# Where a two-layer kernel issues its small transfers: head loads in parts, divisions a step earlier, residual traffic on GpSimd's queue

## The reference

```
xn = layernorm(x)
s  = attention(xn)            # 32 heads of 16, 8 key/value heads (4 query heads share one), full softmax over 512 keys, then Wo
g  = silu(W_down(fwht(silu(W_gate(f)) * W_up(f) )))    # f = fwht(xn * signs); hidden size 2048
x  = x + s * g
```

## Time and profile before

| | |
|---|---|
| median of 3 runs | 1369.06 us (1363.61 to 1372.95) |
| profiled execution: time, span | 1365.89 us, 1364.1 us |
| mean granted PE clock | 0.986 |
| PE busy | 1249.3 us (92%) |
| DVE busy | 1046.7 us (77%) |
| ACT busy | 785.3 us (58%) |
| POOL busy | 524.1 us (38%) |
| issues from SP in layer 0 | 128 transposes, 128 + 128 head loads, 16 `xres` loads, 16 `x1` stores |

### The profile page before, as it was taken

One profiled execution on the slowest core, in us unless ns is written; L12 is line 12 of the kernel. 1 busy time (PEld: TensorE's weight loads), 2 busy tenths in 40 slices (PEclk: granted clock), 3 DMA queues, 4 the chain that ended last, 5 costly groups with the idle time before them and its releaser, 6 DMA issues. The chain is left out here.

```text
span 1364.1 us, 23475 instructions
## 1 busy us (share of the span) xinstructions
PE 1249.3 (92%) x8738; PEld 642.2 (47%) x8738; DVE 1046.7 (77%) x1823; ACT 785.3 (58%) x1306; POOL 524.1 (38%) x434
## 2 busy tenths in 40 slices
PE   4877898989998998899869999999999999999998
PEld 2332333334333433333324546855486555855475
DVE  6778876878876887789864985878776976868846
ACT  4776776668865887578546552365334652355431
POOL 3699951113201221123112762237331772228431
PEclk9989999999999999999989999999999999999999
DMA  6765554676677766777973024002311024001121
GB/s 235 225 144 98 100 98 82 132 154 129 125 128 159 136 118 131 154 141 131 219 216 139 13 59 82 25 24 60 49 46 40 9 71 83 18 31 48 36 41 47
DMA packets 346561, 135.59 MB, mean 99 GB/s; under 512 B 312176, under 2 KB 333392, under 8 KB 343888
## 3 DMA queue, kind: packets, MB, share of 16 engines
q1 hardware_dynamic: 334032, 132.52, 43.5%
q10 hardware_dynamic: 12416, 1.57, 1.1%
HBM read 44.87 MB, written 17.87 MB: 46 GB/s over the span
## 5 line engine op out<-in xcount | busy, mean ns | idle before, releaser
L1178 PE MATMUL bank<-rows,both 128*128 128x512 f16 x1024 | 241.6, 381 | 18.5 <-DVE th L665 9.8
L954 ACT ACTIVATE probs<-vpair,top_n 128x512 f16<-128x512 f32 x256 | 169.9, 686 | 135.0 <-DVE top_n L646 121.3
L646 DVE TENSOR_REDUCE top_n<-vpair 128x1 f32<-128x512 f32 x256 | 169.7, 684 | 77.7 <-PE bank L1147 77.6
L1192 PE MATMUL bank<-dn,h 128*128 128x512 f16 x768 | 186.0, 391 | 0.0
L1178 PEld LDWEIGHTS bank<-rows,both 128*128 128x128 f16 x1024 | 94.6, 98 | 151.1 <-DVE th L665 20.9
L954 ACT ACTIVATE probs<-bank,top_n 128x512 f16<-128x512 f32 x256 | 164.1, 687 | 0.0
L646 DVE TENSOR_REDUCE top_n<-bank 128x1 f32<-128x512 f32 x256 | 163.4, 679 | 0.0
L462 POOL TENSOR_TENSOR h<-th,h 128x512 f16<-128x512 f32 x61 | 70.5, 1156 | 162.9 <-ACT h L923 162.9
L2259 PE MATMUL bank<-rows,both 128*128 128x512 f16 x512 | 118.5, 382 | 0.0
L1192 PEld LDWEIGHTS bank<-dn,h 128*128 128x128 f16 x768 | 72.4, 100 | 96.3 <-issue 23.2
L2275 PE MATMUL bank<-both,hid 128*128 128x512 f16 x512 | 111.2, 379 | 0.0
(11 more groups left out here) (357 smaller groups left out, 2548.8 us busy)
## 6 DMA issues: line engine op xcount, KB each, us to landing
h<-in_ug SPq DMA_DIRECT2D x8, 1024.0 KB, 7.0
lt_scratch<-big SPq DMA_DIRECT2D x16, 384.0 KB, 2.8
dn<-in_down SPq DMA_DIRECT2D x2, 2048.0 KB, 11.5
x_scratch<-th SPq DMA_DIRECT2D x16, 256.0 KB, 2.8
res<-x_scratch SPq DMA_DIRECT2D x16, 256.0 KB, 4.2
out_x<-res SPq DMA_DIRECT2D x16, 256.0 KB, 2.0
both<-in_w SPq DMA_DIRECT2D x2, 1548.0 KB, 8.1
t_scratch<-tok SPq DMA_DIRECT2D x16, 192.0 KB, 2.1
```

The costliest lines, as they stand in the source:

```text
L646: v.tensor_reduce(top_n[:, i:i + 1], SC_[n % G][:, :], AX.X, ALU.max, negate=True).then_inc(S["max_done"], 1)
L954: a.activation(probs[:, k % TAKEN, j * T:(j + 1) * T], SC_[j][:, :], ACT.Exp, bias=top_n[:, i:i + 1]).then_inc(S["p_ready"], 1)
L1178: mm = pe.matmul(GB[n % 2][:, :], w[:, kt, col:col + P], xnb(b, kt), start=r == 0, stop=r == 2 * KT - 1)
L1192: mm = pe.matmul(bk, h16(ft, r // 2)[:, rows], dn16(ft, r % 2), start=j == 0 and r == 0, stop=j == FT - 1 and r == 2)
```

## The change

- `DIVIDE_STEP` goes from 7 to 6: reciprocals and divisions follow `to_tokens` in the same step, ahead of the next pair's maxima.
- `to_features` comes behind `scale_down` in its step (it was ahead of it).
- `ahead` is 0 for m >= 32: in the gate and up stage `scores` and `weigh` come before all matmuls of the step.
- SP's head loads are split: `load_k` of heads 0 to 2 at step 6 as before, head 3 two steps later with head 0 of `load_q`; heads 1 to 3 of `load_q` where all four were.
- The 16 `xres` loads and 16 `x1` stores are issued by POOL, at the same `t`, at the end of POOL's step.

```
-TOKEN_STEP, DIVIDE_STEP, TURN_BACK = 6, 7, 0
+TOKEN_STEP, DIVIDE_STEP, TURN_BACK = 6, 6, 0
...
                 if ta % STEPS == 6 and 1 < ta // STEPS + 2 < NU:
-                    load_k(ta // STEPS + 2)
+                    load_k(ta // STEPS + 2, (0, 1, 2))
+                if ta % STEPS == 0 and 1 < ta // STEPS + 1 < NU:
+                    load_k(ta // STEPS + 1, (3,))
+                if ta % STEPS == 0 and 1 < ta // STEPS + 1 < NU:
+                    load_q(ta // STEPS + 1, (0,))
                 if ta % STEPS == 2 and 1 < ta // STEPS + 1 < NU:
-                    load_q(ta // STEPS + 1)
-                if b >= 0 and m in XRES_STEP:
...
-                if b >= 0 and m - 3 in out_step(b + 1):
...
@@ block.gpsimd @@
                     residual((b - 1) * TT + out_step(b).index(m - 2))
+                if b and m in XRES_STEP:
+                    tt = XRES_STEP.index(m)
+                    n = (b - 1) * TT + tt
+                    if n >= 2:
+                        pool.wait_ge(S["x1_ready"], n - 1)
+                    pool.dma_start(xres[:, tt % 2, :], d["x"][b - 1, tt * P:(tt + 1) * P, :]).then_inc(S[f"xres_in{tt % 2}"], 16)
+                if b and m - 3 in out_step(b):
+                    tt = out_step(b).index(m - 3)
+                    n = (b - 1) * TT + tt
+                    pool.wait_ge(S["x1_ready"], n + 1)
+                    pool.dma_start(x1_dram[b - 1, tt], x1[:, tt % 2, :]).then_inc(S[f"x1_out{tt % 2}"] if n < NT - 2 else W["x1_last"], 16)
@@ block.vector @@
-                if ta % STEPS == TURN_BACK and 0 <= ta // STEPS - 2 < NU and ta // STEPS % 2:
-                    to_features(ta // STEPS - 2)
...
                 if b and m in DOWN_END:
                     scale_down((b - 1) * TT + DOWN_END.index(m))
+                if ta % STEPS == TURN_BACK and 0 <= ta // STEPS - 2 < NU and ta // STEPS % 2:
+                    to_features(ta // STEPS - 2)
@@ block.tensor @@
-                ahead = 1 if ta % 4 == 1 else 0
+                ahead = 1 if ta % 4 == 1 and m < FFN_STEP else 0
```

More of the change, by code:

```diff
@@ L299, in _, with load_k @@
             load_chunk(1)
-            def load_k(u):
+            def load_k(u, heads):
                 b, g, slot = u // NKV, u % NKV, u % SLOTS
@@ L308, in load_k, with load_q @@
                     sp.wait_ge(S["s_ps"], (u - SLOTS + 1) * SC)
-                for j in range(G):
+                for j in heads:
                     sp.dma_start(ks[32 * j:32 * j + DH, slot, :], kst[DH * g:DH * g + DH, :]).then_inc(S[f"heads_in{slot}"], 16)
-            def load_q(u):
+            def load_q(u, heads):
                 slot = u % SLOTS
@@ L358, in _ @@
             for u in range(2):
-                load_k(u)
-                load_q(u)
+                load_k(u, range(G))
+                load_q(u, range(G))
             sp.dma_start(wsd[:, :], d["wscale_dp"].partition_broadcast(P)).then_inc(S["wo_in"], 16)
@@ L382, in _ @@
                 if ta % STEPS == 6 and 1 < ta // STEPS + 2 < NU:
-                    load_k(ta // STEPS + 2)
-                if ta % STEPS == 2 and 1 < ta // STEPS + 1 < NU:
-                    load_q(ta // STEPS + 1)
-                if b >= 0 and m in XRES_STEP:
[L387 to L391, removed]
-                if b >= 0 and m - 3 in out_step(b + 1):
[L393 to L396, removed]
+                    load_k(ta // STEPS + 2, (0, 1, 2))
[3 more added lines that the diff above has]
+                    load_q(ta // STEPS + 1, (0,))
+                if ta % STEPS == 2 and 1 < ta // STEPS + 1 < NU:
+                    load_q(ta // STEPS + 1, (1, 2, 3))
             sp.wait_ge(S["x1_out0"], 16 * (NT // 2 - 1))
```

## The result

The changed kernel takes 1347.54 us, the median of 4 runs (1345.91 to 1347.74), against 1368.88 us (1363.61 to 1372.95, 4 runs): a ratio of 0.9844, 95% interval 0.9809 to 0.9878. Its profiled execution took 1347.46 us, with a span of 1345.6 us, 18.5 us less than before.

A forecast was written before the change was run, and what follows sets the result against it. The prediction took a loop of scores, maxima and exponentials in layer 0 as the bound, delayed by late transposes from SP's full queue. Terms summed to -27.0 us: 1369.06 - 27.0 = 1342 us, range 1335 to 1351 (0.69).

The forecast's parts named there:

- rival 1: SP's queue stays the bound through remaining transposes and head loads: +3 us in each of three repetitions, 1351 us; chance 0.15.
- the stalls at m = 29: Down stage: ACT waits 3.34 us for `probs`, PE 2.94 for `probsT`; both go, round falls from 7.94 to 3.68 us.
- Traffic to POOL and heads split: Down stage, mainly m = 29: SP loses six issues, transpose lateness falls from 6.4 to about 2 us; term 13.3 us.
- Rival 2: POOL's issues are dear: at 5 us each they delay `low_rows` and the last blocks, about +17, 1359 us; chance 0.09.
- Heads split: SP's head loads: 2 of 8 issues leave the transpose after the key loads (0.6 us); nothing is issued less.
- m = 33, -1.75 us: Gate and up stage: scores no longer wait for `scale_down` to empty its bank; round 5.53 down to 3.8 us.
- Ahead pairs: Other gate and up pairs with `weigh`: -0.27 us at the scores, +0.12 or +0.21 before the next; net about -0.1 each.
- Earlier division: Rounds at m = 1, 17 and 49 shorten by 0.86, 0.34 and 0.57 us; a bare reciprocal costs +0.3.
- Batches: Layer 0, batches 1, 2 and 3: terms sum to -8.2, -9.1 and -7.6 us.
- Batch 0, -1.5: Down-weight transforms rule its rounds, so only a few gaps lie open: -1.5 us, with 0 and -4 as ends.
- End of layer 0, -0.6: `divide` of the last unit (0.66 us) falls into a wait of DVE for ACT: -0.6 us.
- Rival 3: Transposes land up to 2 us later, whoever issues, as POOL's transfers overlap them: about +19, 1388 us; chance 0.07.

The follow-up runs named there:

- idle issues: Changed kernel, with SP issuing unneeded loads of 8 bytes a partition where it had issued the residual traffic, which stays on POOL: 1355.16 us, ratio 0.9909.
- reordered end: Changed kernel with `next_split()` taken ahead of `weight_max(1)` on DVE at the end of layer 0: 1346.05 us, ratio 0.9839.

## Why the prediction came out right, and where it did not

The forecast was -27.0 us, the measurement -21.3 in the medians and -18.5 in the profiled executions. By place, in the profiled executions: 22.4 us less in batches 1 to 3 up to unit 31 (forecast 24.9), 1.9 more in batch 0 (1.5 less), 0.6 more at the end of layer 0 (0.6 less), 1.4 more in layer 1 (nothing). The time lies in the forecast's own range, and the loop of the earlier trace rows is what the profile after shows. The number alone proves little: 1347.5 lies 5.5 us above the forecast and 3.5 below the 1351 of rival 1. What decides is that the stalls at m = 29 are gone in all three batches. By the steps of the prediction:

1. *What bounds.* Right. The time that issues hold SP's queue made the transposes late. The idle issues bring the stall back with next to no bytes and no waits.
2. *Traffic to POOL and heads split, -13.3 us.* Right: 13.3 for the two without the rest, 13.1 for the traffic alone. An issue costs 0.54 to 0.59 us of POOL in the middle part, nearer the lower bound of 0.33 than the 1 us taken, with DVE busy 86% of the stretch. Rival 2 (dear issues) did not occur. The 3100 ns that the prediction cited from the Trainium skill, page "SBUF — State Buffer", section "SBUF: two separate sides", are those of a whole transfer and not of its issue, so they are to be held against the time to landing. In the changed kernel POOL's loads and stores landed after a median of 4.5 and 4.0 us, SP's before after 3.1 and 2.8; but in the kernel with traffic and heads alone the same issues from POOL landed after 2.7 and 2.6. So coming from POOL does not by itself make a transfer later here; what made it so in the changed kernel is open. The Trainium skill, page "DMA: Bandwidth & Descriptors", section "Issuing engines are not separate DMA queues", calls the time that another issuer saves usually small against the transfer. An issue of this traffic by SP took 0.33 to 1.09 us, indeed less than its landing; but the term that the prediction said would go by the rule's letter was there, 13.1 us, since the queue had no gap.
3. *Heads split, "0.6 us", nothing credited.* This is the step that failed most, though the total hid it. Alone it is worth 10.0 us, on top of the traffic's move 0.2, and in the whole change 14.0 in the one execution profiled (3.3 by the ratios, 8.9 by the medians). I counted how much lateness one transpose loses, as if the backlog began elsewhere. The bunches of four build it, too. And I costed the parts against the pace of the kernel before; with the rounds of the whole change SP keeps up only with the split. That the change as a whole had both cures is luck as far as this step goes: by my sum the split could have been left out. This also makes rival 1 (SP stays the bound) nearly right: it names what does happen when either half of the cure is missing (+7.4 us, +14.0 us). Its price was too high for its own words: half of 4.26 us is 2.1, not 3, in each repetition.
4. *m = 33, -1.75 us "the scores no longer wait for `scale_down`", "together with the next point".* Right in size (5.53 to 3.77 us, and with the next pair, which pays for the matmul put behind, 10.61 to 3.77 + 5.30 = 9.07), wrong in the main cause: the order on DVE does it; scores first has no part in it when the order is there, and alone it gives 0.75 us.
5. *Ahead pairs, net -0.1.* Right: 0.17 to 0.26 us of gap closed (0.27 forecast), rounds of 4.44 against 4.40. For 7 pairs in 3 batches -0.1 is -2.1 us; measured 1.6 and 1.9. Part of it comes from the reciprocal: it costs 0.06 us behind scores first (4.43 us against 4.37 in the kernel with scores first alone) and 0.22 with the matmul ahead (4.76 against 4.54), where +0.3 was forecast.
6. *Earlier division.* Right at m = 1 (3.67 against 3.68), m = 17 (4.22 against 4.2) and m = 49 (4.44 against 4.40).
7. *Batches.* -6.9, -8.7 and -6.6 (to unit 31) against -8.2 (its terms sum to -8.3), -9.1 and -7.6. Batch 1 lacks 0.9 us at m = 33, where a `weigh` waits 0.8 us for a transpose that is 4.1 us late: two signs of the prediction failed there, the lateness below 3 us and no `weigh` that waits.
8. *Batch 0, -1.5.* Measured +1.9. Of this 1.3 us is there at 48 us, before any changed instruction has run. In batch 0 the clock dips in some of the profiled executions: from 150 to 155 us the kernel with the division alone was granted 0.66, and the changed one 1.00. The start of batch 1 varied from 243.7 to 251.0 us over the kernels. A gain of 1.5 us there can be neither shown nor refused.
9. *End of layer 0, -0.6.* DVE's unbroken chain there starts at 650.88 us instead of 672.73, 21.9 sooner; layer 1's first matmul comes at 714.97 instead of 734.85, only 19.9 sooner. From unit 31's first scores on, 0.6 us were lost instead of 0.6 gained: 1.4 gained before that chain and 2.0 lost from its start, by a wait that I did not forecast: the load of the weight's second half is not sooner by as much, since SP issues it behind transposes held by bulk loads (2.4 us). The hand-off to layer 1 (from POOL's last `residual` to its first instruction of layer 1) also grew, from 3.81 to 4.29 us, with POOL's last store in it.
10. *Rival 3 (later landings).* Landing did lengthen, for stores from a median of 2.8 to 4.0 us, and for transposes in the middle part up to 8.2 us, where 6.4 was the longest; their median stayed at 4.4 to 4.5. The lower lateness covers it.

## What to carry over

When an issuing queue has no gap, ask how late each issue is and where the backlog starts; issues that carry no data hurt as much as real ones, and the order of the issues ahead of the one with a deadline counts as much as their number. Two cures for one backlog do not add: alone they may each look sufficient, and after another edit has quickened the loop both may be needed, so take a part out of the whole as well as testing it alone. After a speed-up, look for the load that does not start sooner: it becomes the next wait.

## What the runs showed of the hardware

- A DMA issued by POOL held it 0.54 to 0.59 us in 30 of 32 cases, with DVE busy 86% of the middle part beside them; the first of all took 0.86 us and the first at the end of layer 0 took 0.74. A store whose data POOL had just made started up to 0.41 us after that operation. Over the layer, by line:

```profile
L516 POOL DMA_DIRECT2D xres<-in_x x16 | 9.5, 591 | 3.5 <-issue 3.5
L521 POOL DMA_DIRECT2D x_scratch<-th x16 | 9.2, 572 | 3.6 <-POOL th L460 3.6
```

- A transpose issued by SP mostly held its queue 1.7 to 2.1 us in a slack queue, 2.6 to 4.7 as the second one behind four loads in the changed kernel without the split, and 12.9 us for two of them behind bulk loads. Once it was 4.5 us in the changed kernel, too, behind three loads and another transpose.
- A load of 8 bytes a partition cost SP as much queue time (0.42 to 1.75 us, median 0.58) as one of a 128x512 block (0.43 to 1.01 us, median 0.45).
- Behind a wait of 9.00 us PE was granted 0.50, the lower of its two clocks (1.2 GHz): 4 matmuls of `project_o` took 1.87 us, and 1.03 us at full clock (2.4 GHz). Behind waits near 3 us both happened: in the kernel before, the 16 matmuls of `weigh` took 1.05 us behind 2.94 us and 0.62 us behind a wait of 3.09 us at 675.69 us. How soon the full clock returned differed: the next 12 matmuls took 3.30 us behind the wait of 9.00 us, 4.32 behind one of 10.44 us in the kernel before, and 4.75 behind one of 6.63 us in the kernel with the reordered end. So the length of the wait alone does not decide it; what does was not tried.
